# Self-attention walked batch by batch, and a residual held in seven tiles of 128 tokens

## The chip, the cores and the metric

The kernel runs on one core of one Trainium2 chip. The metric is the device time of one execution in microseconds. Engines: PE (matrix multiplication), DVE (vector), ACT (scalar), POOL (GpSimd) and SP, which issues the DMAs. Each runs its own instructions in program order; between engines there are only semaphores.

## What is computed

A decoder layer over 8 batches of 112 tokens of width 512 (896 tokens in all), with a layer norm after each of three blocks:

```python
def _L0_attn_ref(x, wq, wk, wv, wo):          # 16 heads of 32
    scores = einsum('bihd,bjhd->bhij', q, k) * scale
    scores = where(idx[None, :] - idx[:, None] > 32, -inf, scores)
    attn = softmax(scores)
    return einsum('bhij,bjhd->bihd', attn, v).reshape(b, s, d) @ wo.T
...
x = _layernorm(x + self_attention(x))
x = _layernorm(x + cross_attention(x, ctx))   # 16 heads of 128, 375 context rows of 256 per batch, RMS norm of q and k
x = _layernorm(x + experts(x))                # a shared expert and the best 2 of 8
```

## The kernel before

Everything is fp32. Where precision counts, an operand is split in a high part (rounded) and a low part (the rest), and a product is made of three matmuls (`three_products`, L84 to L88): high x high, high x low, low x high. ACT or POOL makes the high part, DVE the low one.

The program is three blocks with a barrier between them: `self_attention`, `cross_attention` and `experts`.

**Self-attention** (L150 to L494). The 16 heads are taken as 4 quads of 4. A unit is one quad of one batch; there are N = 32 units, and before the change unit u is quad u // 8, batch u % 8: all batches of a quad, then the next quad. Units are pipelined in slots; slot s does on each engine:
- PE: the four scores of unit s into `scores_ps`, the four transposes of the probabilities of unit s - 3 into `probsT_ps`, the output projection of unit s - 4 into `y_ps` (three matmuls, 112 tokens by 512), half a projection of the next quad into `proj_ps` (six matmuls of 448 columns), and the four products with V of unit s - 3 into `o_ps`.
- DVE: `oT_lo` of unit s - 4, the row sums and reciprocals of unit s - 2, mask add (L387) and row maximum (L391) of unit s, and the addition of y to the residual of unit s - 4 (L400). In the last 8 units the batch statistics of the norm follow (L98, L100).
- POOL: scales the probabilities of unit s - 2 (L273) and subtracts the maximum of unit s (L279).
- ACT: `oT_hi` of unit s - 4 (L326), the copy of `probsT` of unit s - 3 (L331), exp of unit s - 1 (L336), projection copies and weight splits.

The values V of all 8 batches are computed first, in the head and in slots 0 to 2. The context of the next block is split into `ctx_hi` and `ctx_lo` in slots 0 to 23. The residual `resid` has a row of 112 tokens per batch, so 8 tiles, and gets an addition for each of the 32 units.

**Between self- and cross-attention.** The statistics of the 8 tiles are there; POOL's power (L107, L109), DVE's apply (L115) and the turning of the normed rows into `xT_hi` and `xT_lo` (`turn_stages`, L121 to L143: four transposes, an ACT copy, a DVE subtraction per tile) stand at the start of cross-attention. There DVE does `wk_lo`, then the first unit's k statistics and `k_hat`, then the eight turns, then `wq_lo` (L562), on which the first queries wait.

**Cross-attention** (L497 to L1033). 8 pairs of heads by 8 batches, 64 units, in slots again. In each, PE projects k (three parts), turns it, does the output projection of unit s - 5 (six matmuls of 512 columns) between the second and the third part of k, then scores, transposes, and the context products. At the end of each such output projection DVE adds it to the residual tile of that batch.

**Experts** (L1036 on). The residual is normed and turned as above; SP copies it with 14 DMAs from `resid` (8 tiles of 112) into `rows` (7 tiles of 128), from which POOL scatters rows to the experts' places. `resid` then takes what is gathered back.

Names used below: `hold`/`wait` put a semaphore wait in front of the next instruction.

## Time and profile before

| what | us |
|---|---|
| three runs, median (lowest, highest) | 1204.36 (1202.34, 1205.1) |
| the profiled execution, its own time | 1207.62 |
| its span, first to last instruction | 1205.9 |
| PE busy in it | 1102.7 (91%) |
| DVE busy | 672.2 (56%) |
| ACT busy | 464.5 (39%) |
| POOL busy | 442.6 (37%) |

The three blocks lie at 0 to 167, 167 to 881 and 881 to 1206 us. In the rows further down a line of the timeline begins with its start and its length in us; then engine, source line, operation, destination<-sources, shapes, and in brackets how long the engine was idle before it and who released it. Busy time counts a matmul to its modelled end, and matmuls overlap; how long a group of them holds PE is read from the start of one group to the start of the next. A mean hides stages: the 91% of PE is nearly 100% in cross-attention and much less elsewhere.

### The profile page before, as it was taken

The numbers are of one execution on the slowest core, as the hardware profiler recorded it, in microseconds if no ns is written. First come the engines' busy times: TensorE is split into PE (matmuls) and PEld (weight loads), VectorE is DVE, ScalarE is ACT, GpSimd is POOL, SyncE is SP. The second block draws the span as 40 slices with busy tenths as digits, with TensorE's granted clock in tenths as the row PEclk, the third lists the DMA queues.
The fourth block names the chain that finished last, engine by engine and source line by source line (L and its number), as shares of the span: only waits on it lengthen the run. The fifth ranks groups of instructions, "written<-read, shape, count | busy, mean of one in ns | idle before, by whom it ended". The sixth has DMA issues, their size and how long they took to land. (4 is left out here: it accounts for less than half of the span.)

```text
span 1205.9 us, 19600 instructions
## 1 busy us (share of the span) xinstructions
PE 1102.7 (91%) x7034; PEld 931.3 (77%) x7034; DVE 672.2 (56%) x1186; ACT 464.5 (39%) x934; POOL 442.6 (37%) x410
## 2 busy tenths in 40 slices
PE   6988856999999999999999999999849799999994
PEld 5666535899999999999999999998738665566583
DVE  3678852567766766666667667666652211111246
ACT  4444411555554454455454544554321011111200
POOL 0456630665533533535335335333123500000172
PEclk9999955999999999999999999999969899999997
DMA  7120020232322323223213232222173579999432
GB/s 252 36 78 2 2 77 27 87 138 96 126 95 89 105 85 100 95 83 104 91 71 111 92 99 104 77 76 78 52 240 132 235 278 332 349 344 331 187 97 96
DMA packets 45751, 155.27 MB, mean 129 GB/s; under 512 B 3881, under 2 KB 3881, under 8 KB 42641
## 3 DMA queue, kind: packets, MB, share of 16 engines
q1 hardware_dynamic: 43456, 147.21, 35.1%
q0 software_dynamic: 2240, 7.34, 1.8%
q8 instruction: 33, 0.54, 0.2%
q14 instruction: 22, 0.17, 0.0%
HBM read 130.04 MB, written 22.66 MB: 127 GB/s over the span
## 5 line engine op out<-in xcount | busy, mean ns | idle before, releaser
L803 DVE TENSOR_TENSOR xa_kT_lo<-xa_turn_ps,xa_kT_hi 128x750 fp32r<-128x750 f32 x64 | 60.2, 940 | 121.1 <-ACT xa_kT_hi L731 121.1
L694 POOL TENSOR_TENSOR xa_probs<-xa_probs,xa_inv_sum 112x750 f32<-112x750 f32 x64 | 98.7, 1543 | 69.6 <-DVE xa_inv_sum L852 69.6
L86 PE MATMUL xa_k_ps<-xa_wk_hi,ctx_hi 128*125 128x256 f32 x384 | 112.0, 292 | 10.5 <-DVE xa_wk_lo L562 9.8
L679 POOL TENSOR_TENSOR xa_k_ms<-xa_k_ss,xa_sum_eps 125x6 f32<-125x6 f32 x64 | 12.8, 200 | 265.2 <-DVE xa_k_ss L818 265.0
L87 PE MATMUL xa_k_ps<-xa_wk_hi,ctx_lo 128*125 128x256 f32 x384 | 109.8, 286 | 0.0
L88 PE MATMUL xa_k_ps<-xa_wk_lo,ctx_hi 128*125 128x256 f32 x384 | 109.8, 286 | 0.0
L1559 PE MATMUL ex_gu_ps<-ex_raw,ex_xb 128*128 128x352 f32 x336 | 103.0, 459 | 0.7 <-ACT ex_xb L1284 0.7
L924 PE MATMUL xa_c_ps<-xa_probsT_hi,xa_nat 125*128 125x224 f32 x384 | 93.1, 276 | 3.6 <-ACT xa_probsT_hi L747 3.6
L925 PE MATMUL xa_c_ps<-xa_probsT_hi,xa_nat 125*128 125x224 f32 x384 | 92.9, 275 | 0.0
L682 POOL TENSOR_TENSOR xa_k_inv<-xa_k_ms,neg_half 125x6 f32<-125x6 f32 x64 | 85.0, 1328 | 8.4 <-POOL xa_k_ms L679 6.7
L753 ACT ACTIVATE xa_probs<-xa_scores_ps,xa_bias,xa_q_scale 112x375 f32<-112x375 f32 x128 | 83.9, 660 | 10.2 <-DVE xa_bias L828 7.0
L1559 PEld LDWEIGHTS ex_gu_ps<-ex_raw,ex_xb 128*128 128x128 f32 x336 | 62.2, 190 | 32.0 <-ACT ex_xb L1284 0.9
L86 PEld LDWEIGHTS xa_k_ps<-xa_wk_hi,ctx_hi 128*125 128x125 f32 x384 | 73.5, 191 | 15.0 <-issue 11.2
L727 ACT ACTIVATE xa_k_sq<-xa_k_ps 125x512 f32<-125x512 f32 x64 | 38.3, 599 | 114.1 <-PE xa_k_ps L88 114.1
L924 PEld LDWEIGHTS xa_c_ps<-xa_probsT_hi,xa_nat 125*128 125x128 f32 x384 | 73.9, 192 | 4.6 <-issue 4.2
L747 ACT CAST xa_probsT_hi<-xa_turn_ps 125x672 fp32r<-125x672 f32 x64 | 46.1, 720 | 78.7 <-PE xa_turn_ps L998 78.6
L87 PEld LDWEIGHTS xa_k_ps<-xa_wk_hi,ctx_lo 128*125 128x125 f32 x384 | 73.6, 192 | 2.7
L925 PEld LDWEIGHTS xa_c_ps<-xa_probsT_hi,xa_nat 125*128 125x128 f32 x384 | 74.1, 193 | 0.4
L88 PEld LDWEIGHTS xa_k_ps<-xa_wk_lo,ctx_hi 128*125 128x125 f32 x384 | 73.4, 191 | 0.0
L1186 POOL TENSOR_TENSOR ex_up_lo<-ex_raw,ex_up_hi 128x704 fp32r<-128x704 f32 x4 | 6.6, 1675 | 177.0 <-ACT ex_up_hi L1265 177.0
L1448 DVE TENSOR_TENSOR ex_h_blk<-ex_silu_g,ex_gu_ps 128x352 f32<-128x352 f32 x21 | 11.0, 521 | 104.3 <-ACT ex_silu_g L1302 104.3
L818 DVE TENSOR_REDUCE xa_k_ss<-xa_k_sq 125x6 f32<-125x768 f32 x64 | 60.9, 951 | 13.7 <-ACT xa_k_sq L735 11.5
(261 smaller groups left out, 3066.5 us busy)
## 6 DMA issues: line engine op xcount, KB each, us to landing
xa_nat<-ctx_split SPq DMA_DIRECT2D x56, 750.0 KB
ex_raw<-in_w_units SPq DMA_DIRECT2D x23, 1408.0 KB, 7.6
ex_raw<-in_w_units SPq DMA_DIRECT2D x23, 768.0 KB, 6.7
ctx_split<-xa_nat SPq DMA_DIRECT2D x8, 750.0 KB
sorted_x<-ex_y_sb SPq DMA_DIRECT2D x1, 5376.0 KB, 17.7
ex_x_nat<-sorted_x SPq DMA_DIRECT2D x21, 256.0 KB, 6.1
sorted_y<-ex_y_sb SPq DMA_DIRECT2D x21, 256.0 KB, 6.3
xa_wq_raw<-in_w_pairs SPq DMA_DIRECT2D x8, 512.0 KB, 10.4
```

Of the source, the lines that this page charges most:

```text
L86: pe.matmul(out, st_hi, mv_hi, start=first, stop=False)
L87: pe.matmul(out, st_lo, mv_hi, start=False, stop=False)
L88: return pe.matmul(out, st_hi, mv_lo, start=False, stop=last)
L682: pool.tensor_tensor(k_inv[0:KT, :], k_ms[0:KT, :], env["neg_half"][0:KT, 0:2 * KT_N], ALU.pow).then_inc(sem["kinv_done"], 1)
L694: pool.tensor_tensor(probs[0:T, u % 2], probs[0:T, u % 2], inv_sum[0:T, u % 2, :].unsqueeze(2).broadcast_to([T, 2, KV]), ALU.mult).then_in ...
L747: act.copy(probsT_hi[0:KT], turn_ps[0:KT, :, 0:KT_N * T]).then_inc(sem["probsT_hi_done"], 1)
L753: act.activation(probs[0:T, u % 2, h, :], scores_ps[0:T, h, 0:KV], ACT.Exp, bias=bias[0:T, u % 2, h:h + 1], scale=q_scale[0:T, u % B // HA ...
L803: dve.tensor_tensor(kT_lo[:, :, 0:KV], turn_ps[:, :, 0:KV], kT_hi[:, :, 0:KV].bitcast(F32), ALU.subtract).then_inc(sem["kT_lo_done"], 1)
L818: dve.tensor_reduce(k_ss[0:KT, :], k_sq[0:KT, :].rearrange("p (a d) -> p a d", d=XA_DH), AX_X, ALU.add).then_inc(sem["kss_done"], 1)
L924: pe.matmul(c_view[:, c], nat[0:KT, u % 2, 0, at], probsT_hi[0:KT, :, cols], start=(t == 0), stop=False)
L925: pe.matmul(c_view[:, c], nat[0:KT, u % 2, 1, at], probsT_hi[0:KT, :, cols], start=False, stop=False)
L1559: mm = pe.matmul(gu_ps[:, n % 2, half, 0:HID], xb[:, d * P:(d + 1) * P], raw[:, u % RING, w], start=(d == 0), stop=(d == DC - 1))
```

## The change

In self-attention the units are taken batch by batch: unit u is batch u // 4, quad u % 4.
- The projections of all four quads come first: four in the head, twelve whole ones in slots 0 to 3 (`PROJ`, `PROJ_SLOTS`), into `proj_ps` and `y_ps` by turns. `qT` and `kT` hold all quads.
- The values of batch 0 come in the head, those of batch b in two halves in slots 4b and 4b + 1, all into `proj_ps`; V keeps three batches.
- The head outputs `oT` of all four quads are kept, and the output projection runs over 128-token tiles: tile t = b - 1 in the units of batch b, accumulated over the four quads in `y_ps`, 28 groups of three matmuls for 32. DVE adds it to the residual once per tile, 7 times for 32.
- In the slots after that, one step each: statistics and aggregate, POOL's power, apply, turn. Turning uses `proj_ps` too.
- The scores-to-output pipeline is a slot shorter before V: row sums of unit s - 1, transposes of unit s - 2.
- Splits of q and k weights stand before the loop and in slot 2; wo is split in slots 3 to 6 into the room of the q and k weights; wv is split into the room of the context. The context is split in slots 8 to 14 and 31 to 37.

In cross-attention the power, apply and turns are gone from its start. Its output projection runs over the same seven tiles; the slot of batch 1 has none. In the experts the norm and the turn run over seven tiles, the 14 DMAs go, and `got` receives the gathers.

```diff
-    def turn(pe, b):
-        pe.wait_ge(norm_done, b + 1)
-        if b >= 2:
-            pe.wait_ge(sem["turn_lo"], b - 1)
+    def turn(pe, t):
+        pe.wait_ge(norm_done, t + 1)
+        if t >= n:
+            pe.wait_ge(sem["turn_lo"], t - n + 1)
...
+        PROJ = [(0, 0, 0), (0, 0, 1), (0, 1, 0), (0, 1, 1), (1, 0, 0), (1, 0, 1), (1, 1, 0), (2, 0, 0), (2, 0, 1), (1, 1, 1),
+                (2, 1, 0), (2, 1, 1), (3, 0, 0), (3, 0, 1), (3, 1, 0), (3, 1, 1)]
+        PROJ_SLOTS = {0: (4, 7), 1: (7, 10), 2: (10, 15), 3: (15, 16)}
+        ctx_slots = {8: 0, 10: 1, 12: 2, 14: 3, 31: 4, 33: 5, 35: 6, 37: 7}
+        wo_slots = {3: 0, 4: 1, 5: 2, 6: 3}
...
+        def ends_tile(u):
+
+            b, q = divmod(u, QUADS)
+            return b - 1 if q == QUADS - 1 and 1 <= b < B else None
...
+            load_w("wq", 3)
+            load_w("wk", 3)
+            sp.wait_ge(sem["wv_lo_done"], DC)
+            sp.dma_start(wo_raw[:], w_quads[:, :, 2, :].rearrange("q p n -> p q n")).then_inc(sem["wo_loaded"], 16)
+            sp.dma_start(resid[:], x).then_inc(sem["x_loaded"], 16)
+            sp.wait_ge(sem["xT_lo_done"], 2 * DC)
+            sp.dma_start(ctx_raw, ctxT[:, :, 0:HALF * KV]).then_inc(sem["ctx_loaded"], 16)
...
+                t = ends_tile(s - 5)
+                if t is not None:
+                    power(t)
...
+                t = ends_tile(s - 4)
+                if t is not None:
+                    if t == 0:
                         wait(dve, "x_loaded", 16)
+                    wait(dve, "y_ready", QUADS * (t + 1))
+                    dve.tensor_tensor(resid[:, t, :], resid[:, t, :], y_ps[:], ALU.add).then_inc(sem["y_added"], 1)
+                t = ends_tile(s - 5)
+                if t is not None:
+                    wait(dve, "y_added", t + 1)
+                    dve.bn_stats(st[:, t, :], resid[:, t, :]).then_inc(sem["ln_stat"], 1)
+                    wait(dve, "ln_stat", t + 1)
+                    dve.bn_aggr(mv[:, t, :], st[:, t, :]).then_inc(sem["ln_mean"], 1)
...
+                t = ends_tile(s - 7)
+                if t is not None:
+                    turn_low(dve, t)
...
+                    if q == 0:
+                        wait(pe, "y_added", t)
+                        wait(pe, "proj_copied", len(PROJ))
+                    three_products(pe, y_ps[:], oT_hi[:, q, tile_cols(t)], oT_lo[:, q, tile_cols(t)], wo_part(qk_hi, q),
+                                   wo_part(qk_lo, q), q == 0, q == QUADS - 1).then_inc(sem["y_ready"], 1)
...
+                t = ends_tile(s - 7)
+                if t is not None:
+                    wait(pe, "v_copied", min(t + 4, B))
+                    turn(pe, t)
```

and in cross-attention:

```diff
-            ln_power(pool)
...
-            ln_apply(dve)
...
-                    for b in range(B):
-                        turn(pe, b)
-                    pe.wait_ge(sem["turn_lo"], B)
...
+                    t = tile_of(u)
+                    if t is not None:
+                        hold(pe, sem["wo_lo_done"], i, 1, u // B + 1)
+                        hold(pe, sem["oT_lo_done"], i, HALF, u // 2 + 1)
+                        part = slice(t * P, (t + 1) * P)
```

The order on PE in a self-attention slot with a projection, before (sa_wo is the output weight, sa_qk the q and k weights):

```order
L463 MATMUL sa_probsT_ps<-ident,sa_probs 112x112 x4
L86 MATMUL sa_y_ps<-sa_wo_hi,sa_oT_hi 112x512
L87 MATMUL sa_y_ps<-sa_wo_hi,sa_oT_lo 112x512
L88 MATMUL sa_y_ps<-sa_wo_lo,sa_oT_hi 112x512
L86 MATMUL sa_proj_ps<-xT_hi,sa_qk_hi 128x448
L87 MATMUL sa_proj_ps<-xT_hi,sa_qk_lo 128x448
L88 MATMUL sa_proj_ps<-xT_lo,sa_qk_hi 128x448
L86 MATMUL sa_proj_ps<-xT_hi,sa_qk_hi 128x448
L87 MATMUL sa_proj_ps<-xT_hi,sa_qk_lo 128x448
L88 MATMUL sa_proj_ps<-xT_lo,sa_qk_hi 128x448
L490 MATMUL sa_o_ps<-sa_probsT,sa_V 32x112 x4
L452 MATMUL sa_scores_ps<-sa_kT,sa_qT 112x112 x4
```

and now, from the end of a half of values into the slot with a turn (sa_qk holds wo by then; L132 turns a normed tile):

```order
L88 MATMUL sa_proj_ps<-ctx_lo,xT_hi 112x512
L553 MATMUL sa_scores_ps<-sa_kT,sa_qT 112x112 x4
L86 MATMUL sa_y_ps<-sa_qk_hi,sa_oT_hi 128x512
L87 MATMUL sa_y_ps<-sa_qk_hi,sa_oT_lo 128x512
L88 MATMUL sa_y_ps<-sa_qk_lo,sa_oT_hi 128x512
L574 MATMUL sa_o_ps<-sa_probsT,sa_V 32x112 x4
L582 MATMUL sa_probsT_ps<-ident,sa_probs 112x112 x4
L132 MATMUL sa_proj_ps<-ident,resid 128x128 x4
L553 MATMUL sa_scores_ps<-sa_kT,sa_qT 112x112 x4
```

The output projection stands ahead of the products with V now, the transposes behind them, and the projection's place is taken by values or a turn.

The order on DVE in two slots of the loop, before:

```order
L374 TENSOR_TENSOR sa_oT_lo<-sa_o_ps,sa_oT_hi 128x112
L379 TENSOR_REDUCE sa_row_sum<-sa_probs 112x4
L382 RECIPROCAL sa_inv_sum<-sa_row_sum 112x4
L387 TENSOR_TENSOR sa_masked<-sa_scores_ps,sa_mask 112x448
L391 TENSOR_REDUCE sa_row_max<-sa_masked 112x4
L400 TENSOR_TENSOR resid<-resid,sa_y_ps 112x512
```

and now, the slot with a tile's statistics and the two after it:

```order
L477 BN_STATS ln_stats<-resid 128x6
L479 BN_AGGR ln_mv<-ln_stats 128x2
L447 TENSOR_TENSOR sa_masked<-sa_scores_ps,sa_mask 112x448
L451 TENSOR_REDUCE sa_row_max<-sa_masked 112x4
L459 TENSOR_TENSOR sa_oT_lo<-sa_o_ps,sa_oT_hi 128x112
L464 TENSOR_REDUCE sa_row_sum<-sa_probs 112x4
L467 RECIPROCAL sa_inv_sum<-sa_row_sum 112x4
L483 TENSOR_SCALAR resid<-resid,ln_mv,ln_rstd 128x512
L447 TENSOR_TENSOR sa_masked<-sa_scores_ps,sa_mask 112x448
...
L467 RECIPROCAL sa_inv_sum<-sa_row_sum 112x4
L141 TENSOR_TENSOR xT_lo<-sa_proj_ps,xT_hi 128x4x128
L447 TENSOR_TENSOR sa_masked<-sa_scores_ps,sa_mask 112x448
```

Each slot has one step of a tile instead of a residual addition, and the mask add of the next unit stands behind it.

DVE from the end of self-attention into cross-attention (behind the branches), before:

```order
L115 TENSOR_SCALAR resid<-resid,ln_mv,ln_rstd 112x512 x8
L562 TENSOR_TENSOR xa_wk_lo<-xa_wk_raw,xa_wk_hi 128x512
L818 TENSOR_REDUCE xa_k_ss<-xa_k_sq 125x6
L840 TENSOR_TENSOR xa_k_hat<-xa_k_ps,xa_k_inv 125x512
L844 TENSOR_TENSOR xa_k_hat<-xa_k_ps,xa_k_inv 125x256
L140 TENSOR_TENSOR xT_lo<-xa_scores_ps,xT_hi 128x4x112 x8
L562 TENSOR_TENSOR xa_wq_lo<-xa_wq_raw,xa_wq_hi 128x1024
```

and now, with the last steps of the last tile ahead of the branch:

```order
L483 TENSOR_SCALAR resid<-resid,ln_mv,ln_rstd 128x512
L141 TENSOR_TENSOR xT_lo<-sa_proj_ps,xT_hi 128x4x128
L497 TENSOR_TENSOR ctx_lo<-sa_xT_raw,ctx_hi 128x2x375
L158 UNCONDITIONAL_BRANCH
L883 UNCONDITIONAL_BRANCH
L660 TENSOR_TENSOR xa_wk_lo<-xa_wk_raw,xa_wk_hi 128x512
L926 TENSOR_REDUCE xa_k_ss<-xa_k_sq 125x6
L948 TENSOR_TENSOR xa_k_hat<-xa_k_ps,xa_k_inv 125x512
L952 TENSOR_TENSOR xa_k_hat<-xa_k_ps,xa_k_inv 125x256
L660 TENSOR_TENSOR xa_wq_lo<-xa_wq_raw,xa_wq_hi 128x1024
```

The eight applies and the eight turns that stood ahead of `wk_lo` and of `wq_lo` are gone from there.

## Rows read from the trace of the kernel before

**Rows 1.** Busy time by stretch: length, busy us (count) of each engine, PEclk, DMA, GB/s.

```profile
134.00:140.00 6.00, 5.09 (x57) 2.81 (x55) 5.83 (x15) 3.86 (x9) 4.04 (x5) 1.00 0.01 3
...
140.00:151.00 11.00, 7.45 (x69) 4.38 (x61) 10.58 (x25) 3.97 (x9) 5.76 (x7) 0.85 0.01 2
...
290.00:850.00 560.00, 555.94 (x4117) 530.38 (x4117) 382.43 (x634) 278.06 (x568) 239.22 (x208) 0.99 0.28 93
```

**Rows 2.** Timeline of one late self-attention slot, all engines.

```profile
137.49 0.62 DVE L391 TENSOR_REDUCE sa_row_max<-sa_masked 112x4 f32<-112x448 f32 x1
...
137.60 0.46 PE L452 MATMUL sa_scores_ps<-sa_kT,sa_qT 32*112 32x112 f32 x8
...
138.00 0.60 PE L463 MATMUL sa_probsT_ps<-ident,sa_probs 112*112 112x112 f32 x4
...
138.02 0.68 DVE L400 TENSOR_TENSOR resid<-resid,sa_y_ps 112x512 f32<-112x512 f32 x1
...
138.62 0.27 DVE L374 TENSOR_TENSOR sa_oT_lo<-sa_o_ps,sa_oT_hi 128x112 fp32r<-128x112 f32 x1
...
138.63 0.53 ACT L331 COPY sa_probsT<-sa_probsT_ps 112x448 f32<-112x448 f32 x1 [0.78 <-PE sa_probsT_ps L463]
...
138.80 0.61 DVE L379 TENSOR_REDUCE sa_row_sum<-sa_probs 112x4 f32<-112x448 f32 x1
...
138.99 0.46 PE L86 MATMUL sa_y_ps<-sa_wo_hi,sa_oT_hi 128*112 128x512 f32 x1 [0.39 <-DVE sa_oT_lo L374]
...
139.70 0.93 POOL L273 TENSOR_TENSOR sa_probs<-sa_probs,sa_inv_sum 112x448 f32<-112x448 f32 x1 [0.58 <-DVE sa_inv_sum L382]
...
139.83 0.40 PE L490 MATMUL sa_o_ps<-sa_probsT,sa_V 112*32 112x112 f32 x8
...
140.19 0.62 DVE L391 TENSOR_REDUCE sa_row_max<-sa_masked 112x4 f32<-112x448 f32 x1
...
140.30 0.25 ACT L326 CAST sa_oT_hi<-sa_o_ps 128x112 fp32r<-128x112 f32 x1 [0.57 <-PE sa_o_ps L490]
...
140.69 0.59 PE L463 MATMUL sa_probsT_ps<-ident,sa_probs 112*112 112x112 f32 x4
```

**Rows 3.** Timeline, DVE: the row maximum of unit 11 and the mask add of unit 31.

```profile
78.72 0.62 DVE L391 TENSOR_REDUCE sa_row_max<-sa_masked 112x4 f32<-112x448 f32 x1
...
150.39 0.61 DVE L387 TENSOR_TENSOR sa_masked<-sa_scores_ps,sa_mask 112x448 f32<-112x448 f32 x1
```

**Rows 4.** Timeline, PE: first matmuls of the values of batches 0 and 1.

```profile
21.88 0.39 PE L86 MATMUL sa_y_ps<-sa_wv_hi,xT_hi 128*112 128x512 f32 x1
...
24.66 0.39 PE L86 MATMUL sa_proj_ps<-sa_wv_hi,xT_hi 128*112 128x512 f32 x1
```

**Rows 5.** Timeline: from the start of cross-attention to wq_lo.

```profile
167.57 0.10 POOL L647 MEMSET xa_kT_hi<- 128x2 f32 x1 [8.94 <-POOLq L156]
...
170.69 1.04 POOL L81 TENSOR_TENSOR xa_wk_hi<-xa_wk_raw,zero 128x512 fp32r<-128x512 f32 x1 [0.97 <-DMA xa_wk_raw<-in_w_pairs]
...
175.04 0.55 PE L86 MATMUL xa_k_ps<-xa_wk_hi,ctx_hi 128*125 128x256 f32 x1 [9.42 <-DVE xa_wk_lo L562]
...
182.66 0.41 DVE L844 TENSOR_TENSOR xa_k_hat<-xa_k_ps,xa_k_inv 125x256 f32<-125x256 f32 x1
...
182.99 1.15 DVE L140 TENSOR_TENSOR xT_lo<-xa_scores_ps,xT_hi 128x448 fp32r<-128x448 f32 x2
...
191.32 1.22 DVE L562 TENSOR_TENSOR xa_wq_lo<-xa_wq_raw,xa_wq_hi 128x1024 fp32r<-128x1024 f32 x1
```

**Rows 6.** Timeline, POOL: a power over three columns in the experts.

```profile
1191.18 0.89 POOL L109 TENSOR_TENSOR ln_rstd<-ln_rstd,neg_half 128x3 f32<-128x3 f32 x1
```

**Rows 7.** Timeline of a cross-attention slot around its output projection.

```profile
385.90 0.48 PE L86 MATMUL xa_y_ps<-xa_wo_hi,xa_oT_hi 128*112 128x512 f32 x1
...
387.00 0.94 DVE L803 TENSOR_TENSOR xa_kT_lo<-xa_turn_ps,xa_kT_hi 128x750 fp32r<-128x750 f32 x1 [1.68 <-ACT xa_kT_hi L731]
...
387.37 0.28 PE L86 MATMUL xa_k_ps<-xa_wk_hi,ctx_hi 128*125 128x256 f32 x1
```

More of the change, by code:

```diff
@@ L268, in _, with power @@
                                pattern=[[0, QUAD], [-1, T]], channel_multiplier=1).then_inc(sem["consts_set"], 1)
-            for s in range(N + 2):
+            def power(t):
+                part = rstd[:, t:t + 1]
+                wait(pool, "ln_mean", t + 1)
+                pool.tensor_scalar(part, mv[:, t:t + 1, 1], LN_EPS, None, ALU.add).then_inc(sem["ln_eps"], 1)
+                wait(pool, "ln_eps", t + 1)
+                pool.tensor_tensor(part, part, half[:, t:t + 1], ALU.pow).then_inc(sem["ln_pow"], 1)
+            for s in range(SLOTS):
                 u = s - 2
@@ L309, in _ @@
+                act.copy(V[0:T, b % 3, :], proj_ps[0:T, :]).then_inc(sem["v_copied"], 1)
+            split_hi("wq", 0)
+            split_hi("wk", 0)
             for c in range(DC):
                 wait(act, f"xT_{c}_loaded", 16)
-                act.copy(xT_hi[:, c, :], xT_raw[:, c, :]).then_inc(sem["xT_hi_done"], 1)
+                for g in range(2):
+                    cols = slice(g * HT, (g + 1) * HT)
+                    act.copy(xT_hi[:, c, cols], xT_raw[:, c, cols]).then_inc(sem["xT_hi_done"], 1)
@@ new lines, in _ @@
+                u = s - 3
+                if 0 <= u < N:
+                    b, q = divmod(u, QUADS)
+                    wait(pe, "probsT_copied", u + 1)
+                    wait(pe, "v_copied", b + 1)
+                    wait(pe, "oT_lo_done", u)
+                    for r in range(QUAD):
+                        head = q * P + r * SA_DH
+                        mm = pe.matmul(o_ps[r * SA_DH:(r + 1) * SA_DH, 0:T], V[0:T, b % 3, head:head + SA_DH],
+                                       probsT[0:T, u % 2, r * T:(r + 1) * T], start=True, stop=True)
+                    mm.then_inc(sem["o_ready"], 1)
@@ L473, in _ @@
-                half = half_projection(s)
-                if half is not None:
-                    q, p, second = half
-                    wait(pe, ("wq", "wk")[p % 2] + "_lo_done", q + 1)
-                    if not second:
-                        wait(pe, "proj_copied", 4 * q + p)
-                        wait(pe, "v_copied", 6)
-                    for c in (2 * second, 2 * second + 1):
-                        mm = project(proj_ps, p, c, c == 0, c == DC - 1)
-                    if second:
-                        mm.then_inc(sem["proj_ready"], 1)
@@ L484, in _ @@
[L484 to L492 removed]
+                for n in range(*PROJ_SLOTS.get(s, (0, 0))):
+                    project_all(n)
@@ L494, in self_attention @@
+                b, part = divmod(s, QUADS)
+                if 1 <= b < B and part < 2:
+                    values(b, (2 * part, 2 * part + 1))
+                t = ends_tile(s - 7)
+                if t is not None:
+                    wait(pe, "v_copied", min(t + 4, B))
+                    turn(pe, t)
     return sorted(handle.num for handle in sem.values())
@@ L1409, in add_shared @@
                     dve.wait_ge(sem["combined"], 2 * t + 2)
-                dve.tensor_tensor(rows[:, t, :], rows[:, t, :], y_ps[:, n % 2, :], ALU.add).then_inc(sem["y_taken"], 1)
+                dve.tensor_tensor(resid[:, t, :], resid[:, t, :], y_ps[:, n % 2, :], ALU.add).then_inc(sem["y_taken"], 1)
             def take(j):
@@ L1474, in _ @@
         def _(pe):
-            for b in range(B):
-                turn(pe, b)
-            pe.wait_ge(sem["turn_lo"], B)
+            for t in range(TILES):
+                turn(pe, t)
+            pe.wait_ge(sem["turn_lo"], TILES)
             def logits_T():
```

448 lines of the change are left out of this document (232 added, 216 removed).

## The prediction

> **What bounds the kernel now.** Read the busy shares by stretch first [rows 1]. In the last self-attention slots PE is neither full nor idle: 5.09 of 6 us from 134 us on, then 7.45 of 11 us, and in that second stretch the mean granted clock falls to 0.85. From 290 to 850 us, the cross-attention, PE is busy 555.94 of 560 us: there every PE microsecond counts. Next the timeline of one slot that has no projection left, all engines [rows 2]. DVE starts a row maximum at 137.49 and the next at 140.19, 2.70 us later, back to back: DVE is the bound there. The same maximum starts at 78.72 for unit 11 and at 137.49 for unit 27, and the mask add of unit 31 starts at 150.39 [rows 2, 3]: 58.77 us for 16 units, 3.67 us each. So while projections are interleaved a slot costs about 1 us more than DVE needs. Cross-attention begins with a chain through POOL, DVE and PE [rows 5] in which nothing is full.
>
> I count slots from 0; M is the start of a unit's mask add on DVE. The sum is made against the profiled execution, 1207.6 us (span 1205.9), 3.3 us over the median of 1204.4.
>
> **Start to unit 11.** Twelve 512-column matmuls (one batch of values) take 24.66 - 21.88 = 2.78 us [rows 4]; twelve of 448 columns so take about 2.43 (estimate by columns). PE may begin after half a chunk of xT, about 1 us sooner, and ends the first four projections near 20.9, values of batch 0 near 23.7. Slots 0 to 3 then hold twelve whole projections, 29.2 us, and wait once 0.8 us for the value copy. With scores, transposes and outputs slot 4 starts near 56.6. Slots 4 to 7 have no output projection yet and take 2.7 us each, slots 7 to 11 about 2.9: M(11) is near 76.9, against 78.72 - 0.64 = 78.1 before. **-1.2 us.** SP's queue changes too: the weights of quads 1 to 3 now stand ahead of wo, x and the context, and SP waits there for wv_lo and xT_lo. None of these is wanted before slot 3 (wo), 8 (context) and 11 (x), tens of microseconds later, so I cost it at nothing; if that cover were gone, it would be one landing of x. Cross-check: by unit 11 PE has done seven projections more (17.0), five values less (13.9) and four output projections less (3.4), so nearly the same work.
>
> **Units 11 to 31.** What DVE loses is large: the residual add once per four units, not each time (0.60 from its start to the next operation [rows 2]); four slots would cost 4 x 2.10 = 8.4 us, and a tile's add, statistics, apply and xT_lo, four of about the add's size, some 2.6: 11.0 us per batch. PE has per batch four times scores 0.40, output projection 0.84, probs x V 0.40, transposes 0.4 [rows 2], 2.8 of values and 0.5 of turning: about 11.5 us. If only engines bound, a batch would take 11.5 us and not 15. But the new order joins two batches' work in one chain, which I walk from M of the slot with the tile's add:
> - mask, max, oT_lo, sum, reciprocal, then the add: its end is at 2.8. The next output projection overwrites y_ps and waits for it: PE starts it at 2.9, PxV at 3.74, ACT's oT_hi 0.47 later, oT_lo at 4.5, the sum 0.18 later, reciprocal, statistics and aggregate begin by 6.15. Queued behind that PE wait are this slot's outputs, transposes and values.
> - POOL waits for the aggregate in order, ahead of the next unit's probabilities. Epsilon +0.27, power +0.34, then the power itself: 0.89 us on three columns [rows 6], I take 0.6 on one (bounds 0.3 and 0.9). POOL is free at 7.4, its scaling to the transposes takes 140.69 - 139.70 = 0.99 [rows 2]: 8.35.
> - transposes 0.4, half a batch of values 1.4, scores 0.4, output 0.84, outputs of the heads 0.4: the transposes of the third slot at 11.8.
> - the turn of a tile shares proj_ps with the values and must wait for the copy of V, which ACT does after the copy of probsT: 0.63 to that copy, 0.45 more, 0.6 for V: PE turns at 13.5, 0.55; ACT hi 0.6; DVE lo 0.65 (the two of 112 tokens took 1.15 us [rows 5], widened by 128/112). DVE holds the next mask add behind it: M at 15.3.
>
> So a batch takes 15.3 us (3.8 per unit), no better than before. Five batches 76.5, and four context splits some 0.9 of DVE: 77.4 us, against 150.39 - 78.1 = 72.3 before, which had the cheap slots of 2.7 us at its end. **+5.1 us.** Bounds: 11.5 us per batch (engines alone) to 17.
>
> **Tail of self-attention.** From M(31) to the next stage 17.1 us before (POOL starts it at 167.57 [rows 5]). Now the last tile also waits for POOL's power (0.9 with its epsilon), apply, turn, hi and lo, and three late context splits of some 0.9 (DVE takes 0.94 for 750 columns [rows 7]) lie in DVE's way; against that the chain from exp to transposes is a slot shorter. Walked in the same way: 19.5. **+2.4 us** (0 to +5).
>
> **Entry of cross-attention.** Gone from it are the power and apply of eight tiles and eight turns. The weight wk is ready to round at 170.69, 1.04 us long; its low part 0.7 more; PE could start at 172.55 instead of 175.04 [rows 5]. The same chain to the end of k_hat, 7.95 us (182.66 + 0.41 - 175.04 = 8.0), ends at 180.5, and wq_lo starts there instead of at 191.32. **-10.8 us**; what would be late next is POOL's wq_hi, which its place in POOL's queue, now without the eight-column power ahead of it, makes no later. Bounds -9 and -11.5.
>
> **Cross-attention.** Seven output projections in place of eight per pair: six matmuls less in one slot of eight, 387.37 - 385.90 = 1.47 us [rows 7]. But they covered a wait: ACT has kT_hi ready at 387.0, when DVE starts kT_lo, and without them PE asks for it after the third k product, at 386.6: 0.4 stall. kT_lo takes 0.94 to 387.94, PE wants it at 387.7: 0.3 stall. Left 0.7 per pair, eight pairs: **-5.6 us** (bounds 0 and -11.8).
>
> **Experts.** Seven turns for eight, each 128/112 wider, at half clock: about 0 (+-1). The fourteen DMAs from resid to rows on SP go, but POOL's scatter waited for slot numbers, not for them; gathers get a tile of their own. 0.
>
> **Sum**: -1.2 + 5.1 + 2.4 - 10.8 - 5.6 = -10.1: 1197.5 in the profiled execution, 1194.3 against the median.
>
> **Rivals.**
> 1. The loop runs near its engines (12.9 us per batch, if POOL and ACT get ahead of my chain). For it: DVE alone needs 11.0. Against: both waits are in program order. -10.1 - 5 x 2.4 = -22: 1182.
> 2. Slower: PE's clock falls in the new loop. PE works 11.5 of 15.3 us, 75%; the row of 140 to 151 us shows 7.45 of 11, 68%, with a fall, the one before 85% without [rows 1]; 134 to 140 is the nearer in its full slots, the other in its waits. At half clock PE's 11.5 us of work become some 20 (twice, less the fixed latencies; an estimate): +4.8 per batch; over six batches +29: 1223. It decides against the change from 2.1 batches at half clock on. The Trainium skill (TensorE: Matmul & The Clock Gate, "HAM oscillation — how this bites in real kernels") ties the fall to idle gaps of PE that last, and by it a loop with waits of 1.2 and 1.7 us keeps its clock and this rival has no chance. The row of 140 to 151 us does not bear that out.
> 3. Cross-attention gives nothing, its slot being held by kT and k_hat: 1199.9. For it: both covered waits above.
> 4. The waits are longer than counted (17 us per batch: the power at 0.9 and more, PE's late start costs DVE a second time): +8.5: 1202.8. The change then does not do what it says: the norm is in the loop, but the loop pays for it.
>
> **Chances.** Forecast 0.48, rival 1 0.17, rival 3 0.10, rival 4 0.13, rival 2 0.12. Range 1181 to 1206: it reaches to rivals 1 and 4 and the first part of rival 2, and leaves out most of rival 2 and a gain beyond rival 1. A measurement tells some 0.2% from no change, 2.4 us. Faster 0.75, same 0.11 (rival 4, a little of 2), slower 0.14.
>
> **What would show it.** In the new profile: slot 4 near 57 us; mask adds about 15.3 us apart per four units, DVE idle for ACT's xT_hi in one slot of four and for oT_hi in another; POOL's probabilities held behind the power; next stage about 6 us later than 167.5; first queries near 188 instead of 192.7; PE in cross-attention as full as before, 5 to 6 us shorter; experts unchanged. Wrong would make it: batches near 12 or 17 us, or a granted clock near 0.5 before 150 us.

## Result: slower by 0.3%, and the profile after

Over 20 runs of each, the changed kernel takes 1208.9 us (1204.6 to 1212.2) and the kernel before 1204.5 (1201.1 to 1211.7). The ratio is 1.0031, with a 95% interval of 1.0018 to 1.0045. The forecast was 1194.3, with a range of 1181 to 1206: wrong in direction, and outside the range.

The profiled execution took 1211.6 us (span 1209.9), against 1207.6 before. From its page, the span, PE's busy time, and the two rows of the 40 slices (30.2 us each) that matter here:

```profile
span 1209.9 us, 19455 instructions
...
PE 1096.4 (91%) x6966; PEld 927.6 (77%) x6966; DVE 651.6 (54%) x1149; ACT 464.9 (38%) x936; POOL 439.6 (36%) x422
...
PE   6988864899999999999999999999849799999994
...
PEclk9998975899999999999999999999959899999997
```

PE is busy 6 us less than before (1102.7), in line with its fewer matmuls, and the kernel is longer all the same. In the fourth slice, self-attention, the granted clock already shows an 8; the kernel before had 9 there. Busy time by stretch, the last self-attention batches and the tail (columns as in [rows 1]: stretch, its length, busy time of PE, PEld, DVE, ACT, POOL, then granted clock, DMA share, GB/s):

```profile
79.00:97.00 18.00, 14.20 (x132) 8.76 (x131) 15.43 (x31) 9.85 (x21) 10.05 (x12) 1.00 0.00 1
97.00:114.00 17.00, 14.09 (x120) 8.77 (x117) 12.81 (x28) 6.78 (x17) 8.45 (x10) 0.90 0.26 92
114.00:131.00 17.00, 13.71 (x116) 8.42 (x108) 11.98 (x28) 6.93 (x15) 8.60 (x11) 0.90 0.01 1
131.00:148.00 17.00, 13.59 (x108) 8.55 (x108) 11.55 (x27) 6.32 (x14) 8.95 (x11) 0.90 0.01 1
148.00:165.00 17.00, 13.18 (x100) 8.14 (x100) 11.59 (x27) 7.25 (x16) 8.94 (x12) 0.90 0.00 1
165.00:185.00 20.00, 10.20 (x52) 5.95 (x52) 10.42 (x19) 5.52 (x11) 4.39 (x8) 0.56 0.00 1
```

A mean of 0.90 over 17 us is some 3.4 us at half clock (1.2 GHz) and the rest at full (2.4 GHz), once in each of four batches; the batch from unit 11 on (79 to 97 us) has none. Before 79 us there is one more such stretch, near 68 to 72. The kernel before has none ahead of the second stretch of [rows 1]. Now one batch, all engines, from the timeline of the changed kernel (start us, length us, engine, line, operation, what it writes and reads; in brackets the idle time before it and what ended that). It answers to [rows 2] and [rows 3]:

```profile
143.36 0.59 ACT L352 COPY sa_V<-sa_proj_ps 112x512 f32<-112x512 f32 x1
...
144.01 0.66 PE L132 MATMUL sa_proj_ps<-ident,resid 128*128 128x128 f32 x4 [1.11 <-ACT sa_V L352]
...
144.76 0.59 ACT L137 CAST xT_hi<-sa_proj_ps 128x512 fp32r<-128x512 f32 x1 [0.80 <-PE sa_proj_ps L132]
...
145.38 0.69 DVE L141 TENSOR_TENSOR xT_lo<-sa_proj_ps,xT_hi 128x512 fp32r<-128x512 f32 x1 [1.64 <-ACT xT_hi L137]
...
145.98 0.61 DVE L447 TENSOR_TENSOR sa_masked<-sa_scores_ps,sa_mask 112x448 f32<-112x448 f32 x1
...
148.09 0.66 DVE L473 TENSOR_TENSOR resid<-resid,sa_y_ps 128x512 f32<-128x512 f32 x1
...
149.00 0.47 PE L86 MATMUL sa_y_ps<-sa_qk_hi,sa_oT_hi 128*128 128x512 f32 x1 [1.79 <-DVE resid L473]
...
151.15 0.63 PE L87 MATMUL sa_proj_ps<-ctx_hi,xT_lo 128*112 128x512 f32 x1
...
152.82 0.57 POOL L315 TENSOR_TENSOR ln_rstd<-ln_rstd,neg_half 128x1 f32<-128x1 f32 x1
...
153.35 0.94 POOL L321 TENSOR_TENSOR sa_probs<-sa_probs,sa_inv_sum 112x448 f32<-112x448 f32 x1
...
153.41 0.69 PE L553 MATMUL sa_scores_ps<-sa_kT,sa_qT 32*112 32x112 f32 x8
...
155.26 0.59 PE L582 MATMUL sa_probsT_ps<-ident,sa_probs 112*112 112x112 f32 x4
...
162.47 0.61 DVE L447 TENSOR_TENSOR sa_masked<-sa_scores_ps,sa_mask 112x448 f32<-112x448 f32 x1
```

Mask adds of units 27 and 31 start at 145.98 and 162.47: 16.49 us per batch. From the first of them on, the steps lie where the prediction put them up to the power: add at an end 2.8 us later, output projection at +3.0, power done at +7.4. But PE meanwhile works at half clock. The six values matmuls between 150.60 and 153.3 take 0.43 us from start to start, not the 0.23 of full clock. PE comes to the transposes at 155.26, though their probabilities have been ready since 154.3. These transposes are at +9.3; the walk had 8.35. This microsecond is still there at the next mask adds.

The tail and the entry of cross-attention, same view and columns; it answers to [rows 5]:

```profile
169.00 0.82 POOL L313 TENSOR_SCALAR ln_rstd<-ln_mv 128x1 f32<-128x1 f32 x1 [3.33 <-DVE ln_mv L479]
...
170.44 0.94 POOL L321 TENSOR_TENSOR sa_probs<-sa_probs,sa_inv_sum 112x448 f32<-112x448 f32 x1
...
171.43 0.99 PE L582 MATMUL sa_probsT_ps<-ident,sa_probs 112*112 112x112 f32 x4 [1.80 <-POOL sa_probs L321]
...
176.02 0.63 PE L88 MATMUL sa_y_ps<-sa_qk_lo,sa_oT_hi 128*128 128x512 f32 x1
...
176.63 0.93 DVE L497 TENSOR_TENSOR ctx_lo<-sa_xT_raw,ctx_hi 128x750 fp32r<-128x750 f32 x1
177.47 0.68 DVE L473 TENSOR_TENSOR resid<-resid,sa_y_ps 128x512 f32<-128x512 f32 x1
...
183.75 0.93 DVE L497 TENSOR_TENSOR ctx_lo<-sa_xT_raw,ctx_hi 128x750 fp32r<-128x750 f32 x1
...
184.96 0.10 POOL L759 MEMSET xa_kT_hi<- 128x2 f32 x1 [4.30 <-POOLq L158]
...
189.71 0.55 PE L86 MATMUL xa_k_ps<-xa_wk_hi,ctx_hi 128*125 128x256 f32 x1 [7.28 <-DVE xa_wk_lo L660]
...
197.98 1.22 DVE L660 TENSOR_TENSOR xa_wq_lo<-xa_wq_raw,xa_wq_hi 128x1024 fp32r<-128x1024 f32 x1
...
199.25 0.74 PE L86 MATMUL xa_y_ps<-xT_hi,xa_wq_hi 128*128 128x448 f32 x1 [5.37 <-DVE xa_wq_lo L660]
```

Unit 31 to the next stage takes 184.96 - 162.47 = 22.5 us, against 17.2. The new stage to its first queries takes 14.3 us, against 25.1.

Where the time went, between the same points of the two profiled executions:

| stretch | before | after | change | forecast |
|---|---|---|---|---|
| start to unit 11's mask add | 78.1 | 79.9 | +1.8 | -1.2 |
| units 11 to 31 | 72.3 | 82.6 | +10.3 | +5.1 |
| tail of self-attention | 17.2 | 22.5 | +5.3 | +2.4 |
| stage start to first queries | 25.1 | 14.3 | -10.8 | -10.8 |
| first queries to first kT_lo | 21.3 | 21.1 | -0.1 | 0 |
| first to last kT_lo | 644.5 | 640.7 | -3.9 | -5.6 |
| last kT_lo to the end | 347.4 | 348.8 | +1.4 | 0 |
| sum | 1205.9 | 1209.9 | +4.0 | -10.1 |

### The profile page after: what moved, and what is told of

It is laid out like the page before. It is cut to its first block and busy times, and to the rows that moved or that the text cites. A ratio compares the mean times of both kernels' runs of the same rounds, so it can differ in the third digit from the quotient of the medians.

```text
span 1209.9 us, 19455 instructions
## 1 busy us (share of the span) xinstructions
PE 1096.4 (91%) x6966; PEld 927.6 (77%) x6966; DVE 651.6 (54%) x1149; ACT 464.9 (38%) x936; POOL 439.6 (36%) x422
## 5 line engine op out<-in xcount | busy, mean ns | idle before, releaser
L805 POOL TENSOR_TENSOR xa_probs<-xa_probs,xa_inv_sum 112x750 f32<-112x750 f32 x64 | 98.7, 1542 | 70.7 <-DVE xa_inv_sum L960 70.7
L790 POOL TENSOR_TENSOR xa_k_ms<-xa_k_ss,xa_sum_eps 125x6 f32<-125x6 f32 x64 | 12.9, 201 | 258.6 <-DVE xa_k_ss L926 258.6
L86 PEld LDWEIGHTS xa_k_ps<-xa_wk_hi,ctx_hi 128*125 128x125 f32 x384 | 73.8, 192 | 11.6 <-issue 8.7
## 6 DMA issues: line engine op xcount, KB each, us to landing
sorted_x<-ex_y_sb SPq DMA_DIRECT2D x1, 5376.0 KB, 20.9
```

Source lines behind the costliest of these rows:

```text
L86: pe.matmul(out, st_hi, mv_hi, start=first, stop=False)
L805: pool.tensor_tensor(probs[0:T, u % 2], probs[0:T, u % 2], inv_sum[0:T, u % 2, :].unsqueeze(2).broadcast_to([T, 2, KV]), ALU.mult).then_in ...
```

## Experiments

Two theories for the loop. "Clock": what a batch has over the 15.3 us of the walk is the half-clock stretch. "Waits": the chain through add, power and copy of V is itself 16.5 us long. "Clean" below is a batch with no half-clock stretch in it.

### e1: work for PE in its waits

```
+                    wait(pe, "turn_lo", t - 1)
+                    wait(pe, "v_copied", min(t + 2, B))
+                    fill(6, proj_ps)          # 448-column matmuls, results unread
                     wait(pe, "y_added", t)
...
+                    wait(pe, "masked_done", min(s + 1, N))
+                    fill(5, scores_ps[:, 0])
                     wait(pe, "v_copied", min(t + 4, B))
                     turn(pe, t)
```

> The changed kernel with idle-time filler on PE: six 448-column matmuls whose results nobody reads, ahead of the wait for the tile add, and five ahead of the turn's wait for the copy of V. They use banks that nobody reads then, and are about as long (some 0.2 us each at full clock) as PE waits there anyway (1.8 and 1.1 us), so no step of the chain moves. Theory 'clock' (the five stretches of 3.4 us at granted clock 0.5, one per batch, cost the loop what it has over my 15.3 us per batch): the stretches between 70 and 160 us vanish or thin out, a batch of four mask adds takes 15.2 to 15.6 us in place of 16.5, unit 31 starts near 157, and the kernel comes out at 1202 to 1205. Rival 'waits' (the chain through add, POOL power and V copy is itself 16.5 long): batches stay at 16.4 to 16.6 whatever the clock does, time 1208 to 1210.

Measured: 1204.0 us (1202.4 to 1207.2), ratio 0.9982 (0.9959 to 1.0006). Busy time of a stretch, then the mask adds of units 27 and 31:

```profile
72.00:165.00 93.00, 85.93 (x711) 55.42 (x710) 69.29 (x149) 41.04 (x89) 48.96 (x57) 1.00 0.05 18
```

```profile
145.08 0.61 DVE L447 TENSOR_TENSOR sa_masked<-sa_scores_ps,sa_mask 112x448 f32<-112x448 f32 x1
...
160.48 0.61 DVE L447 TENSOR_TENSOR sa_masked<-sa_scores_ps,sa_mask 112x448 f32<-112x448 f32 x1
```

Not one fall from 72 to 165 us, and the last two batches take 15.39 and 15.40. The edit adds work and waits for nothing less, so the clock was the cause of the 1.1 us per batch, and "waits" falls. Other things were not foreseen. The batches from units 11 and 15 on took 16.56 and 16.04 even at full clock: three of the four early context splits stand in them (the first comes before unit 11) and make them 1.8 us longer, where I had 0.9 for all four. The batch from unit 19 on has no split and took 15.73; in it ACT and DVE write the outputs of batch 4 to two places, twice as wide (0.39 us for `oT_lo`, not 0.27), but that this is the reason was not tested. Filler ahead of the first tile, which has no add to wait for, cost 1.3 us (units 7 to 11: 14.23 instead of 12.94). So unit 31 came at 160.5, not near 157. And the tail behind it took 23.8 us, 1.3 more than in the changed kernel; e4 shows why.

### e2: the power behind the next unit's probabilities

```
                                        ALU.mult).then_inc(sem["probs_done"], 1)
+                t = ends_tile(s - 6)
+                if t is not None:
+                    power(t)
...
-                t = ends_tile(s - 5)
-                if t is not None:
-                    power(t)
```

> The changed kernel with POOL's power of a tile moved behind the scaling of the next unit's probabilities, so these wait 0.9 us less. Theory 'clock': in a batch with a half-clock stretch PE reaches those transposes at 155.25, 0.8 us after the probabilities are ready, so the power is hidden behind the slow values matmuls: batches stay within 0.2 us of 16.5, time 1207 to 1210. Rival 'waits': the power is on the chain: 15.6 per batch, five batches -4.5 us, time near 1204.

Measured: 1201.4 us (1198.4 to 1205.3), ratio 0.9971 (0.9947 to 0.9994). The three batches with a half-clock stretch took 16.43, 16.62 and 16.48, as "clock" said: there the power is hidden. A clean one took 14.97 (mask adds at 144.30 and 159.27), 0.4 less than in e1; the one from unit 11 on, clean and with two splits in it, took 15.50 instead of 16.56, so there the power had its whole effect. The time was better than either theory gave, for a reason that neither named: the tail fell from 22.5 to 19.7. In part that is because the last unit's probabilities no longer wait for a power (their transposes start 7.3 us behind the mask add of unit 31, not 9.0); the rest is taken up below, under the tail.

### e3: the add ahead of oT_lo, row sum and reciprocal

```
                     split_lo("wk", 3)
+                t = ends_tile(s - 4)
+                if t is not None:
+                    ...                        # the wait for y and the tile add
                 u = s - 3
```

> The changed kernel with the tile add on DVE moved ahead of oT_lo, row sum and reciprocal, so that PE's next output projection can start 0.8 us sooner. Both theories: PE's idle time before that projection falls from 1.8 to about 1.0 us and a batch becomes 0.6 to 0.8 us shorter, -3 to -4 us: near 1205. The clock theory adds that with less idle time the half-clock stretches may go too: then 15 us or less per batch and near 1200; the rival says the rest of the gap stays.

Measured: 1205.2 us (1201.7 to 1206.8), ratio 0.9991 (0.9969 to 1.0012). The clean batch took 14.80, 0.6 less than in e1; those with a stretch took 16.50, 16.22 and 16.13. The time is the one expected; the stretches became fewer by one but did not go.

### e4: filler through the tail and the entry as well

```
+                    fill(5 if t < TILES - 1 else 20, scores_ps[:, 0])
...
                     turn(pe, t)
+                    if t == TILES - 1:
+                        fill(10, scores_ps[:, 0])
...
+                if s == 0:
+                    fill(18)                   # then the first keys
...
                 if s == 0:
+                    fill(24)
                     queries(0, 0)
+                    fill(8)
                     queries(0, 1)
+                    fill(8)
```

> e1 with more filler: 20 and 10 matmuls around the last turn of self-attention, 18 before the first keys of cross-attention, 24, 8 and 8 around its first queries. Theory 'clock': PE works from 167 to 219 us at half clock; with the clock kept, keys (3.9 us), two queries (9.3), square sums (3.1) and second keys (2.7) shrink by up to half, and the tail's matmuls too: 6 to 10 us less than e1, near 1196. Rival (these stretches are bound by DMA, POOL and DVE, PE's clock is worth nothing there): like e1, or 2 to 4 us slower where filler at half clock is longer than the wait it should fill.

Measured: 1201.6 us (1199.5 to 1205.4), ratio 0.9963 (0.9938 to 0.9989); 2.4 under e1, not 6 to 10. The entry did what "clock" says: stage start to first kT_lo 28.4 us against 35.4 in the changed kernel and 32.8 in e1, which kept full clock in part of it. The tail did not get shorter:

```profile
160.00:182.00 22.00, 16.91 (x96) 12.80 (x94) 12.20 (x24) 6.92 (x14) 5.53 (x7) 0.92 0.01 1
```

Here the granted clock is 0.92 and the tail is still 22.6 us. It would be easy to conclude that half clock costs the tail nothing (the expectation of e5 below takes this tail as one at full clock). The timeline does not bear that out, because the filler costs something itself:

```profile
169.76 2.24 PE L507 MATMUL sa_scores_ps<-sa_qk_hi 128*128 128x448 f32 x5
...
170.27 0.27 DVE L459 TENSOR_TENSOR sa_oT_lo<-sa_o_ps,sa_oT_hi 128x112 fp32r<-128x112 f32 x1 [1.84 <-ACT sa_oT_hi L390]
...
171.80 1.06 PE L132 MATMUL sa_proj_ps<-ident,resid 128*128 128x128 f32 x4
...
172.51 0.75 PE L86 MATMUL sa_y_ps<-sa_qk_hi,sa_oT_hi 128*128 128x512 f32 x1
```

The one fall here, from 169.7 to 173.1, meets five unread matmuls. They hold PE for 2.0 us, and the last output projection starts at 172.51 though its `oT_lo` was ready at 170.54. So e4 gives no price of the clock in the tail. The loop was e1's, with e1's flaw at the first tile.

### e5: the late context splits in slots 30 to 33

```
-        ctx_slots = {8: 0, 10: 1, 12: 2, 14: 3, 31: 4, 33: 5, 35: 6, 37: 7}
+        ctx_slots = {8: 0, 10: 1, 12: 2, 14: 3, 30: 4, 31: 5, 32: 6, 33: 7}
```

> The changed kernel with the four late context splits in slots 30 to 33 in place of 31, 33, 35 and 37. From e4's trace, whose tail is at full clock and yet 22.6 us long: two of the splits (0.93 us each on DVE) stand between the last output projection and the last add, and behind the last xT_lo. Theory 'queue' (the tail is long because late operations stand in DVE's and POOL's way, whatever the clock): the tail, mask add of unit 31 to the start of the next stage, goes from 22.5 to 20.7. Rival 'clock' (it is long because PE runs it at half clock): within 0.3 us of 22.5, as DVE then waits for PE instead. Batches before unit 29 as in the changed kernel, 15.4 or 16.5 with a half-clock stretch; time 1205 to 1208.

Measured: 1208.1 us (1202.0 to 1209.6), ratio 1.0011 (0.9989 to 1.0032). The tail took 20.9 us, as "queue" said. In the timeline of the changed kernel, the split at 176.63 holds back the last add, and the one at 183.75 stands between the last xT_lo and the next stage. e5 takes away the second, 0.9 us, and the one beside POOL's last epsilon, which takes 0.22 us here and not 0.82. A split still stands ahead of the last add, which comes 14.9 us behind the mask add of unit 31, not 15.0. The whole time is not told from that of the changed kernel.

### e6, e7, e9: the moves together, with filler, and the copy of V first

e6 is the edits of e2, e3 and e5 in one. e7 adds filler, with the counts of its expectation:

```
+                        if t >= 1:
+                            wait(pe, "turn_lo", t - 1)
+                            wait(pe, "v_copied", min(t + 2, B))
+                            fill(3, proj_ps)
                         wait(pe, "y_added", t)
...
+                    fill(4 if t < TILES - 2 else 20 * (t == TILES - 1), scores_ps[:, 0])
```

e9 makes one new move in the changed kernel:

```
                     act.activation(probs...)
+                b, part = divmod(s - 2, QUADS)
+                if part == 0 and 1 <= b < B:
+                    copy_values(b)
                 u = s - 3                      # oT_hi, then the copy of probsT
...
-                b, part = divmod(s - 2, QUADS)
-                if part == 0 and 1 <= b < B:
-                    copy_values(b)
```

> The changed kernel with the moves of e2 (power behind the scaling), e3 (add ahead of oT_lo) and e5 (splits) together, no filler. Clean batches were 14.97 in e2 and 14.8 in e3 against 15.40 in e1: if these are two links of one chain, the clean batch is 14.3 to 14.4; five batches save some 5 us against clean ones, more where the shorter waits also spare half-clock stretches. Tail 19.7 - 1.8 = 17.9 (e2's less e5's), some 17.5 with the earlier add. Time 1195 to 1199. If the links only hide one another: batch 14.8, tail 19.5, time 1200.

Measured: 1197.2 us (1194.2 to 1201.6), ratio 0.9930 (0.9898 to 0.9963). Batches from unit 19 on 14.71, 14.56 and 14.62, all clean without any filler: shorter waits also spare the falls. The batch before them still had a stretch and took 16.70. The links partly overlap (14.6, not 14.3). Tail 17.0.

> e6 with filler on PE: three matmuls ahead of the wait for the add (not for the first tile, where there is no add to wait for and e1 lost 1.3 us), four ahead of a turn's wait, 20 and 6 around the last turn, 18, 24, 7 and 7 in the entry of cross-attention. Theory 'clock': no half-clock stretch between 75 and 250 us but for one or two; entry from the stage's start to its first kT_lo 28.4 us as in e4 against 35.4 in the changed kernel: 6 to 8 us under e6, time 1187 to 1192. Rival: filler delays as much as it spares; within 2 us of e6.

Measured: 1189.5 us (1188.1 to 1191.5), ratio 0.9873 (0.9840 to 0.9906). Its tail is 17.1 at full clock; e6's 17.0 is at half clock only in its last 5 us. Two things cancel there: behind the last add e7 takes 5.57 us where e6 takes 6.03, and ahead of it e7's filler puts an output projection, and all behind it, 0.6 us later. The entry took 27.0 us instead of 33.1.

> The changed kernel with one move on ACT: the copy of V comes ahead of oT_hi and of the copy of probsT, not behind them, so PE can turn the tile right behind its transposes. If the turn's wait for that copy sets the slot of 4.76 us, as my chain says (copy of V, turn, hi, lo, next mask add), this slot falls to 3.5 and a batch from 16.5 (or 15.4 without a half-clock stretch) by 1.2 us; six batches -7 us, near 1202. Rival (the slot is held by DVE's or POOL's work beside the turn, since without any turn it was still 3.3 us and the batch only 1.05 shorter): the slot falls by 0.3 or less, the next slots take the rest back, time near 1208.

Measured: 1202.0 us (1198.6 to 1205.7), ratio 0.9971 (0.9952 to 0.9990). The slot of 4.76 us fell to 3.43, a clean batch took 14.23; two of the five batches had a half-clock stretch (15.29 and 15.12). The turn's wait for the copy of V was a link, and a mere matter of order on ACT.

### e8: no turns in the loop

The edit in e1's kernel, which leaves the turns out; only the spacing of the mask adds is read, from one execution:

```
-                    turn(pe, t)
...
-                    turn_high(act, t)
...
-                    turn_low(dve, t)
...
-                    wait(pe, "turn_lo", b - 3)
```

> e1 (changed kernel with filler, batches 15.4 at full clock) without the turns of the tiles in the loop: PE's four transposes, ACT's xT_hi and DVE's xT_lo of each tile are left out, so cross-attention works on a transposed input that is not the residual's. It measures what turning inside the loop costs. My chain says the turn stands between the copy of V and the next mask add: the slot of 4.76 us falls to 2.8 to 3.0 and the batch to 13.5. Rival (it lies beside other waits): the batch stays above 14.8. Time not read: only the spacing of the mask adds.

Measured: the last batches took 14.35 us, the slot 3.3. So leaving out the turn saved 1.05 us per batch, not the 1.9 expected. PE's wait for the copy of V is still in this kernel:

```profile
151.92 0.59 ACT L352 COPY sa_V<-sa_proj_ps 112x512 f32<-112x512 f32 x1
...
152.56 0.46 PE L555 MATMUL sa_scores_ps<-sa_kT,sa_qT 32*112 32x112 f32 x8
...
153.09 0.62 DVE L446 TENSOR_TENSOR sa_masked<-sa_scores_ps,sa_mask 112x448 f32<-112x448 f32 x1 [0.80 <-PE sa_scores_ps L555]
```

The scores start as the copy ends (152.51), and the mask add waits for them. So this slot stays at 3.3 instead of the 2.8 to 3.0 expected, and the one behind it became 0.3 longer (3.00 against 2.68). The slot is a chain of both: 4.8 us with the turn behind a late copy of V (e1), 3.3 without the turn (e8), 3.4 with the turn behind an early copy (e9).

### e10 and e12: four moves, with and without filler; e11: filler in the kernel before

e10 is e7 with the edit of e9 and `fill(0 ...)` ahead of the turns; e12 is e10 without filler. e11 edits the kernel before, in the first slot of its cross-attention:

```
+                if s == 0:
+                    fill(28)                   # then the first keys
...
                     for b in range(B):
+                        if b >= 2 and b % 2 == 0:
+                            fill(18 if b == 2 else 2)
                         turn(pe, b)
+                    fill(9)
...
                     queries(0, 0)
+                    fill(7)
                     queries(0, 1)
+                    fill(7)
```

> e7 with the move of e9, and no filler ahead of the turns. If the turn's wait is a link of the chain of its own, a clean batch is 14.7 - 1.2 = 13.5, six of them -7 us: 1183. If DVE's work then bounds (11 us per batch) it does not matter yet. Rival: without the filler the half-clock stretches come back, or the gain is 0.3 per batch: 1188 to 1191.

Measured: 1184.6 us (1183.2 to 1186.4), ratio 0.9838 (0.9815 to 0.9860). The turn of a tile in its timeline:

```profile
131.00 0.59 ACT L352 COPY sa_V<-sa_proj_ps 112x512 f32<-112x512 f32 x1 [0.18 <-PE sa_proj_ps L88]
...
132.94 0.60 PE L132 MATMUL sa_proj_ps<-ident,resid 128*128 128x128 f32 x4
...
134.26 0.69 DVE L141 TENSOR_TENSOR xT_lo<-sa_proj_ps,xT_hi 128x512 fp32r<-128x512 f32 x1 [0.31 <-ACT xT_hi L137]
...
134.86 0.61 DVE L447 TENSOR_TENSOR sa_masked<-sa_scores_ps,sa_mask 112x448 f32<-112x448 f32 x1
```

The copy of V ends 1.35 us before PE turns, and the turn has no wait ahead of it. The last batches took 13.35 and 13.39.

> e10 without any filler: the changed kernel with the four moves (power behind the scaling, add ahead of oT_lo, splits in slots 30 to 33, copy of V first). It separates order from clock. If the moves alone keep the clock in the loop, as in e6 from 100 us on, batches are 13.4 to 13.9 and the tail 17, and only the entry is at half clock: stage start to first kT_lo 33.1 us as in e6 against 26.9 in e10, time 1184.6 + 6.2 = 1190 to 1192. If half-clock stretches come back in the loop, 1.1 us for each: up to 1196.

Measured: 1190.5 us (1188.7 to 1193.8), ratio 0.9865 (0.9825 to 0.9905). Batches 13.25 and 13.29 with the clock at 1.00 from 72 to 148 us, tail 17.0, stage start to first kT_lo 35.4. Order alone keeps the clock in the loop. What e10 has over it, 5.9 us in the medians and 8.1 in the profiled executions, is the entry's (26.9 us there).

> The kernel before the change with the same kind of filler on PE in the entry of cross-attention alone (28 matmuls ahead of the first keys, 18 ahead of the third turn, 9 behind the turns, 7 and 7 around the second query). It shows how much of e7's lead is due to the clock in the entry and not to the change. There the queries, square sums and second keys took 21.3 us at half clock in the kernel before and 14.2 in e7 at full clock: -7, and some 2 for keys and turns: 1196 to 1198 if the clock is kept. Rival (the clock is still down from 147 us on, and filler at half clock is twice as long as its wait): 1203 to 1208.

Measured: 1195.3 us (1193.4 to 1197.3), ratio 0.9917 (0.9891 to 0.9944). Stage start to first kT_lo fell from 46.4 to 37.3 us. So 9 us of the gain over the kernel before need no other change. The like comparison is e10 with e11: 10.7 us for the change once its order is mended. Without filler on either side, e12 against its own runs of the kernel before (1206.6), it is 16.1.

## Why the prediction was wrong

The profiled execution is 14.1 us above the sum (span 1209.9, forecast 1195.8): 3.0 of them up to unit 11, 5.2 in units 11 to 31, 2.9 in the tail, 1.7 in cross-attention, 1.4 behind it. Point by point, against its own steps.

**Entry of cross-attention: right.** -10.8 forecast, 25.1 to 14.3 us measured. wq_lo starts behind the second k_hat, as foreseen.

**Units 11 to 31: the step that failed.** The walk of one batch was right in every link within 0.2 us (15.3 us in all; e1 measured 15.4). What failed is the assumption under it, that PE keeps its clock: rival 2, to which I gave 0.12, was true in part. I had priced it as a loop wholly at half clock, +4.8 us per batch and 1223 in all, and so as improbable. In fact some 3.4 us of a batch were at half clock, in four of the five batches. Against the same batches of e1 they cost 0.4, 0.8, 1.1 and 1.1 us (the last two 16.48 and 16.49 against 15.39 and 15.40): 3.4 of the 5.2 us missed here. The rest is clean batches 0.1 longer than the walk (0.5), context splits dearer (1.8 us for three, not 0.9 for four), and 0.3 in the batch with the wider copies.

The power was mis-sized in its effect: in a clean batch without splits it is worth 0.4 us (e2), not the 0.9 of my walk; behind a half-clock stretch next to nothing.

I had weighed a rule of the Trainium skill (TensorE: Matmul & The Clock Gate, "HAM oscillation — how this bites in real kernels") and noted that by it such a loop keeps its clock. The trace disagrees: the fall came with waits of 1.8 and 1.1 us on PE. A later section of that page of the Trainium skill ("A second HAM failure mode: psum-queue depth-cycling") tells of a kernel in which frequent short idles made the clock swing, and by that one the trace agrees. I had not weighed it.

**Tail: +5.3 instead of +2.4, mechanism missed in part.** The walk had the last tile's power and three late splits. It did not have the power of the tile before, ahead of the last unit's probabilities on POOL, nor half clock. e2 moves that power away and saves 2.8 us: 1.6 of them up to the transposes of those probabilities. The other 1.1 lie between these and the end of the last output projection, where e2 has full clock:

```profile
166.58 0.60 PE L582 MATMUL sa_probsT_ps<-ident,sa_probs 112*112 112x112 f32 x4
...
170.03 0.40 PE L88 MATMUL sa_y_ps<-sa_qk_lo,sa_oT_hi 128*128 128x512 f32 x1
```

That is 3.45 us, and from 171.43 to 176.02 in the changed kernel, in the same order on every engine but POOL, 4.59. The tails of e4 and e7, at nearly full clock and yet no shorter, say nothing against it: in both, filler took what the clock gave. The splits are the third part: those behind the last add cost 1.4 (e5), and the one ahead of it was moved by none of the runs. How the 19.5 us of my walk divide among these is not on record, so the shares of the 2.9 missed are not either.

**Start to unit 11: +1.8 instead of -1.2.** Slot 4 began at 57.3 where I had 56.6. Units 4 to 7 took 9.2 us instead of 8.1, units 7 to 11 12.9 instead of 11.6. In these last stand a context split (76.39, 0.9 us), which I had counted behind unit 11, and the first half-clock stretch (68 to 72 us). Two executions, of e5 and e9, had 6.8 us of half clock here instead of 3.4 and took 14.5 and 14.4 from unit 7 to 11; the seven others without filler ahead of the first tile took 12.9 to 13.0. So a second such stretch costs 1.5 here. What the first costs was not measured, since every variant kept it.

**Cross-attention: right per pair.** Starts of kT_lo, eight units apart, after and then before (a pair with no fall in it):

```profile
464.88 0.94 DVE L911 TENSOR_TENSOR xa_kT_lo<-xa_turn_ps,xa_kT_hi 128x750 fp32r<-128x750 f32 x1 [2.29 <-ACT xa_kT_hi L842]
...
546.32 0.94 DVE L911 TENSOR_TENSOR xa_kT_lo<-xa_turn_ps,xa_kT_hi 128x750 fp32r<-128x750 f32 x1 [2.28 <-ACT xa_kT_hi L842]
```

```profile
458.78 0.94 DVE L803 TENSOR_TENSOR xa_kT_lo<-xa_turn_ps,xa_kT_hi 128x750 fp32r<-128x750 f32 x1 [2.29 <-ACT xa_kT_hi L731]
...
540.82 0.94 DVE L803 TENSOR_TENSOR xa_kT_lo<-xa_turn_ps,xa_kT_hi 128x750 fp32r<-128x750 f32 x1 [2.29 <-ACT xa_kT_hi L731]
```

81.44 against 82.04: 0.6 per pair of the 0.7 forecast. The slot that lost six matmuls shrank by 0.7 and not by 1.47; PE has two waits in it that it did not have before, 0.2 us for kT_hi and 0.4 for kT_lo, as worked out. The whole stretch gained 3.9 and not 5.6: the changed kernel had a fall of the clock in three of its pairs, the kernel before in two, and a fall costs 1.55 us. In the runs above, with the same code there, this stretch took 637 to 642 us.

**Experts: no change to be seen.** +1.4 in this pair of executions; the same code took 346.2 to 349.5 us in the others, 348.4 in the mean of all twelve, against 347.4 in both profiles of the kernel before's code. What of that 1 us belongs to the change is not told.

Of rival 4 ("waits longer than counted", 1202.8) the size of the batch nearly came true (16.5, against 17), but for another cause. The sign of the true one, a granted clock near 0.5 before 150 us, was among those that I had named.

## What to carry to other kernels

When a change puts work of two batches in one chain, price the clock as well as the chain. A loop with waits of 1 to 2 us on PE can lose part of each batch at half clock, and shorter waits or unread matmuls in them give it back. Before moving work from an idle stage into a loop, look at each in-order queue that it joins: three moves within POOL's, DVE's and ACT's order, with one of the splits, turned +4 us into -16 (e12 against its runs of before). And where a stage is at half clock, filler is no free test of what the clock costs there: it was worth 6 to 9 us in the entry, but in the loop ahead of the first tile and in the tail its unread matmuls stood ahead of needed ones and took 0.6 to 2 us themselves. Compare the same steps, from start to start, in executions where the clock happened to differ.
